# Who copies a chunk's row numbers into the gather ring: GpSimd in place of ScalarE

## The reference, cut to what matters

```python
agg = segment_sum(x[src], edge_type * N_NODES + dst)      # 8 x 3125 rows of 256
h   = act(einsum('rnd,rde->ne', agg.reshape(8, N, D), W) + x @ root + bias)
```

## Time and profile before

| | |
|---|---|
| median of three runs | 4742.41 us (4733.30 to 4748.82) |
| span of the profiled execution | 4717.6 us |
| median less span | 24.8 us |
| GpSimd busy | 2426.4 us, 51% of the span |
| TensorE busy | 2893.6 us, 61% |
| VectorE busy, ScalarE busy | 1194.6 us and 443.2 us |
| mean granted TensorE clock | 0.767 |

### The profile page before, as it was taken

The page is one execution under the profiler, slowest core; times in us unless marked ns, Lnnn a source line. Parts: engine busy times, 40 slices in busy tenths (PEclk is TensorE's granted clock), DMA queues, the critical chain, the costliest instruction groups (busy, mean ns, idle before and its releaser), DMA issues. The chain is left out here.

```text
span 4717.6 us, 51616 instructions
## 1 busy us (share of the span) xinstructions
PE 2893.6 (61%) x16304; PEld 2587.3 (55%) x16304; DVE 1194.6 (25%) x2874; ACT 443.2 (9%) x1230; POOL 2426.4 (51%) x2564
## 2 busy tenths in 40 slices
PE   2556555555556556655656565656767666767786
PEld 2555555545555445545545464555656566666675
DVE  4222222222222122212212122323333233333322
ACT  1000000000000000000000000001111111111132
POOL 5655555555554555555555545665544444444333
PEclk8777777777777776777777777777878778778898
DMA  6333333333333222222222223323443444444576
GB/s 159 108 97 97 99 98 100 100 100 97 101 106 112 84 76 76 84 80 77 81 81 80 81 66 103 87 86 113 134 149 116 132 136 128 142 136 130 169 240 208
DMA packets 276981, 524.37 MB, mean 111 GB/s; under 512 B 60783, under 2 KB 180331, under 8 KB 276716
## 3 DMA queue, kind: packets, MB, share of 16 engines
q0 software_dynamic: 121152, 331.40, 24.3%
q1 hardware_dynamic: 154396, 190.17, 12.7%
q10 hardware_dynamic: 1296, 1.24, 0.1%
HBM read 458.71 MB, written 63.91 MB: 111 GB/s over the span
## 5 line engine op out<-in xcount | busy, mean ns | idle before, releaser
L677 POOL DMA_INDIRECT arena<-rows_dram,arena x2396 | 2273.7, 949 | 1924.7 <-ACT arena L826 1173.3
L1868 PE MATMUL bank<-arena 128*128 128x128 f32 x4836 | 921.4, 320 | 741.3 <-issue 377.2
L1868 PEld LDWEIGHTS bank<-arena 128*128 128x128 f32 x4836 | 821.1, 229 | 833.9 <-issue 509.2
L1463 DVE TENSOR_TENSOR arena<-arena,bank 128x256 f32 x807 | 339.7, 421 | 2690.7 <-remote 1766.8
L1872 PE MATMUL bank<-arena 128*128 128x128 f32 x4836 | 819.5, 309 | 122.9 <-issue 121.8
L1872 PEld LDWEIGHTS bank<-arena 128*128 128x128 f32 x4836 | 733.2, 223 | 134.2 <-issue 133.8
L1723 PE MATMUL bank<-arena 128*128 128x256 f32 x2400 | 632.6, 405 | 171.0 <-DVE zcol L1358 103.3
L1723 PEld LDWEIGHTS bank<-arena 128*128 128x128 f32 x2400 | 463.6, 206 | 236.7 <-issue 182.5
L1385 DVE TENSOR_TENSOR arena<-bank,arena 128x1408 f32<-128x1408 f32 x222 | 355.5, 1604 | 13.1 <-issue 11.6
L1788 PE MATMUL bank<-arena 128*128 128x256 f32 x576 | 203.7, 530 | 151.4 <-ACT arena L904 119.2
L1788 PEld LDWEIGHTS bank<-arena 128*128 128x128 f32 x576 | 157.0, 280 | 191.5 <-issue 157.7
(11 more groups left out here) (230 smaller groups left out, 1529.1 us busy)
## 6 DMA issues: line engine op xcount, KB each, us to landing
arena<-in_L_ffn_W_dram SPq DMA_DIRECT2D x112, 512.0 KB
arena<-in_L_ffn_W_dram SPq DMA_DIRECT2D x44, 1024.0 KB
arena<-rows_dram,arena POOLq DMA_INDIRECT x2418
xs_dram<-zslot SPq DMA_DIRECT2D x25, 1224.0 KB
arena<-xs_dram SPq DMA_DIRECT2D x56, 136.0 KB
rows_dram<-arena SPq DMA_DIRECT2D x50, 128.0 KB
arena<-in_L_gnn_weights_dram SPq DMA_DIRECT2D x6, 1024.0 KB
arena<-ys_dram SPq DMA_DIRECT2D x8, 640.0 KB, 7.8
```

Of the source, the lines that this page charges most:

```text
L677: nc.gpsimd.indirect_dma_start(out=gath[:, slot, :], out_offset=None, in_=rows_dram[l], in_offset=bass.IndirectOffsetOnAxis(ap=idx_ring[:, ...
L1463: nc.vector.tensor_tensor(acc, acc, edge_bank(l, s, q)[:, 0:KD * WC].rearrange("p (k r n) -> p k r n", k=KD, r=REL), ALU.add).then_inc(S[" ...
L1868: nc.tensor.matmul(edge_bank(l, s, q)[:, 0:WC], gath[:, slot, 0:P], onehot[:, slot, :], start=first, stop=last)
```

## The change

GpSimd's stream gets a `ring` of its own: it waits for `group_mm` itself (and in front of chunk C at the start of layers 1 and 2 for `miss_mm`), copies the chunk's row numbers to the ring with `nc.gpsimd.tensor_copy`, raises `ix_ready`, and then waits for `ix_ready` as before, ahead of the gathers. ScalarE's `ring`, its calls, and the copies L997, L1002 and L1006 go. Chunks 0 and 1 of the first layer stay with ScalarE. VectorE's wait for `ix_ready` (L1427) stays.

```diff
@@ gpsimd
                 with pool.If(outside < 1):
                     wait(pool, "rows_st", 16 * (NT - 1) * l)
 
+                    def ring(s, a, n):
+
+                        used = -(-CH * (a + 1) // GT)
+                        if is_first(s):
+                            freed = GROUPS * (l - 1) + (SG * (NSPAN - 1) - (-CH // GT) if a == 0 else GROUPS) if l > 0 else 0
+                        else:
+                            freed = GROUPS * l + SG * (s.m - 1) + used
+                        wait(pool, "group_mm", freed)
+                        if l > 0 and is_first(s) and a == CPS - 1:
+                            wait(pool, "miss_mm", l)
+                        part = idx_part if l > 0 and is_first(s) and a == 0 else idx_i[:, bass.ds(CH * (CPS * s.m + a), n)]
+                        nc.gpsimd.tensor_copy(idx_ring[:, CH * a:CH * a + n], part).then_inc(S["ix_ready"], 1)
+
                     def span(s):
                         for a, n in chunks_of(s):
                             if l == 0 and is_first(s) and a < AHEAD:
                                 continue
+                            ring(s, a, n)
                             if l > 0 and is_first(s) and a == 1:
 
                                 wait(pool, "last_st", 16 * l)
@@ scalar
-            def ring(l, s, a, half, n):
-
-                q = CPS * s.m + a
-                used = -(-CH * (half + 1) // GT)
-                wait(act, "group_mm", GROUPS * l + (SG * (s.m - 1) + used if a < CPS and not is_first(s) else SG * s.m + used if a >= CPS else 0))
-                nc.scalar.copy(idx_ring[:, CH * half:CH * half + n], idx_i[:, bass.ds(CH * q, n)]).then_inc(S["ix_ready"], 1)
-
@@ scalar, span
-                        if is_first(s):
-                            if l == 0:
-                                for a in range(AHEAD, CPS):
-                                    ring(l, s, a, a, CH)
-                            if l == 1:
-                                mix_exp()
+                        if is_first(s) and l == 1:
+                            mix_exp()
...
-                            if u % CH == CH - 1 and not is_last(s):
-                                a = u // CH
-                                if not (is_int(s.m, NSPAN - 2) and a == 2):
-                                    ring(l, s, a + CPS, a, LAST_CHUNK if is_int(s.m, NSPAN - 2) and a == 1 else CH)
-
@@ scalar, end of layers 0 and 1
                         hidden_rows(l, NT - 2)
-                        wait(act, "group_mm", GROUPS * l + SG * (NSPAN - 1) - (-CH // GT))
-                        nc.scalar.copy(idx_ring[:, 0:CH], idx_part).then_inc(S["ix_ready"], 1)
                         turned_back(l, NT - 2)
                         if l == 1:
                             q_stage(NT - 2)
-                        wait(act, "group_mm", GROUPS * (l + 1))
-                        nc.scalar.copy(idx_ring[:, CH:2 * CH], idx_i[:, CH:2 * CH]).then_inc(S["ix_ready"], 1)
                         hidden_rows(l, NT - 1)
                         act.wait_ge(S["miss_mm"], l + 1)
                         nc.scalar.copy(missed[0:LAST, :], bank[NODE_BANK][0:LAST, :]).then_inc(S["miss_out"], 1)
-                        nc.scalar.copy(idx_ring[:, 2 * CH:3 * CH], idx_i[:, 2 * CH:3 * CH]).then_inc(S["ix_ready"], 1)
                         turned_back(l, NT - 1)
```

## The result

The changed kernel took 4622.16 us (median of 4 runs, 4590.40 to 4638.40), the kernel before 4743.06 beside it (4 runs, 4733.30 to 4748.82). The ratio is 0.9719, 95% interval 0.9680 to 0.9758: faster by 2.8%. The prediction said 4781 us and slower. Later runs showed something the prediction had no place for. On two other chips the same kernel before takes 3384 us instead of some 4700, and on one of them the change was measured: it makes the kernel 4.8% slower there. The document first follows the pair of traces that the prediction was about, then the experiments on both sorts of chip.

A forecast was written before the change was run, and what follows sets the result against it. No engine is full; a loop of waits sets the pace, with handovers waiting for TensorE's groups. Waiting chunks +5, ready chunks +39, ScalarE's order -5 made +39 on 4742.4: 4781 us, own range 4757 to 4835, 8-in-10 range 4715 to 4840.

The forecast's parts named there:

- What a waiting chunk pays: GpSimd's handover at 169 chunks that wait for TensorE's group: 1.13 us before, 1.13 to 1.18 after; +5 us in all.
- What a ready chunk pays: 51 chunks with row numbers already copied, nearly all a span's third: 1.06 us for 0.30 ahead of the gather; +39 us.
- Does each delay reach the end?: A span's three chunks stand in one chain, so a microsecond lost ahead of the third lengthens the span by one.
- held add: VectorE's add of a group computed long before; it was seen 3.30 us behind the third chunk's last gather.
- first rival: Pause ahead of a span's third chunk pays for itself: -83 us, 4659; 14 in 100 clear gain, 20 no change.
- ScalarE's order: Copies held up behind gelus in layer 2 and a copy of `missed` at layer starts are freed: together -5 us.

The follow-up runs named there:

- e10: The changed kernel, unaltered, run again on a late chip beside the kernel before: 4435.94 us, ratio 0.966.
- e12: Changed kernel with the third chunk's row numbers copied during the second, so no pause ahead of a ready third chunk; late chip: 4582.12 us, 0.998.
- e18: Changed kernel with the third chunk's row numbers copied and waited for after the second chunk's sixth gather; late chip: 4549.74 us, 0.966.
- e16: The changed kernel, unaltered, run on a prompt chip beside the kernel before: 3547.95 us, ratio 1.048.
- e2: Changed kernel with ScalarE still waiting for the groups at its old places, without copying: 4649.15 us, 0.979.
- e1: Kernel before plus one GpSimd copy into unused columns and a wait for it ahead of each span's third chunk: 4717.14 us, 0.991.
- e3: Changed kernel with GpSimd copying each chunk's row numbers during the chunk before, into two rings, without pauses: 4682.23 us, 0.986.
- e11: Kernel of e3 plus a GpSimd copy and wait ahead of each span's third chunk, on a late chip: 4492.56 us, 0.977.
- e13: Changed kernel plus a GpSimd copy and wait after the fifth gather of every chunk, on a prompt chip: 3701.45 us, 1.094.
- e7: Changed kernel with the third chunk's row numbers copied during the second, so no pause ahead of it; prompt chip: 3502.76 us, 1.035.
- e4: Changed kernel plus a second GpSimd copy and wait ahead of each span's third chunk: 4616.71 us, 0.970.

## Why the prediction was wrong

**The prices were right.** "What a waiting chunk pays": 1.13 us, forecast 1.13 to 1.18 after, and the group that ends at 1900.69 is followed by the gather at 1901.88, 1.19 behind. "What a ready chunk pays": forecast 1.06 us in front of C, measured 0.96 in layer 0 and 1.04 in layer 1, so +0.66 to +0.74 instead of +0.76. The 0.09 us that I had put ahead of the copy is not there: the copy starts where the gather ends.

**The step that failed is "Does each delay reach the end?"**, in its last sentence but one: "a microsecond lost ahead of C is a microsecond on the span". It took the distance from C's last gather to the held add as fixed. On late chips that distance is what the pause shortens (e10 against e12), and in the first pair, while 46 pauses cost 32 us, the handovers behind them gave back 110. The first rival had this mechanism, with 14 in 100 for a clear gain and 4659 us as its end; the measured 4622 lies beyond even that. Against it I had held that the pause was seen once, and that 1.06 us is shorter than the 2.3 us after which held groups were seen. The second argument was wrong: the pause need not be long enough for the signal to come inside it. In e18 it ends 16 us ahead of the add that it advances. And the effect had been measured too small: the earlier trace rows is the third group's add, 2.30 us behind C's last gather, but the earlier trace rows is the second group's, 3.30 behind; the third group's stood 4.12 behind.

**The same step is right on a prompt chip.** There VectorE's adds follow their groups, all three chunks are ready, and the forecast price of 0.76 us on 220 chunks would be +167 us. Measured: +163 (3384.65 to 3547.95). That they meet so closely is partly luck: the traces show some 0.70 us a chunk, 154 us, and the kernel before has no trace on such a chip to show where the rest is. The trace that I read had the sign of the chip in it: VectorE waiting for something that the profile could not name. That row of the kernel before, of the changed kernel, and of e16 on a prompt chip:

```profile
DVE arena L1463 <- remote: 1766.8, 218, 19.3
```

```profile
DVE arena L1456 <- remote: 1710.9, 243, 15.2
```

```profile
DVE arena L1456 <- PE bank L1865: 1771.6, 637, 11.6
```

I wrote that I did not know why the groups' semaphores are seen so late, and went on to price the change as if the lateness were a constant. A wait whose cause is unknown should have had both bounds in the sum: held fast, +39; moved by the change, -83 or more. The range (4715 to 4840) reached only part of the way to the second.

**ScalarE's order** was forecast at -5 us. By e2 it may be as much as 30 on a late chip, a quarter of the gain; the intervals do not tell the two apart, and the two ratios are from two chips.

**What stays open.** Why a pause ahead of C is worth 3.2% between e12 and e10, but only 0.9% on the kernel before (e1) and 0.8% between e3 and e11 (two chips). These differ in who copies at A's and B's handover, and no run changed that alone. Breaks in every chunk (e13) were not measured on a late chip. The changed kernel ran on two late chips and on one prompt chip, and the prompt one has no trace of the kernel before. And why late chips are late is not shown.

## What to carry to other kernels

Where an engine stands idle although its producer's work is recorded as long done, find out what the wait follows before pricing a change by it. Here it followed the bursts of gathers, and for pauses of 0.7 us in bursts of 22 three times their length came back. Time such a change on more than one chip: this one is worth -2.8 and -3.4% on two late chips and +4.8% on a prompt one, and a tuning that fits one sort undoes the other. Where nothing is held, a copy and an own wait in GpSimd's stream cost 0.7 us for each chunk, and the relay over an idle ScalarE costs nothing.

## What the runs showed of the hardware that I had not expected

Two sorts of chips, or of states of them. On chips 2 and 4 the kernel before took 3381 to 3386 us, elsewhere 4567 to 4778. Instructions last the same on both: a gather on GpSimd 0.952 us in the changed kernel's first trace and 0.950 in e7's, an add 0.421 in both. TensorE is busy 2900.6 us in the changed kernel's first trace and 2892.8 in e16's, so its granted clock (0.766 and 0.844 in the mean) is not the difference. The difference is in the signals. On a late chip the mean lag from group to add is 4.8 to 6.8 us in layers 0 and 1, up to 25; on a prompt one 0.3, at most 1.7 (in layer 2 4 to 5 on the one and 1.0 on the other). The late traces also hold fewer records of signals: 16,756 semaphore updates in the kernel before and 17,151 in the changed one, 52,634 in e16. The row of the gathers in the list of DMA issues (count, then the median time to landing where there is one), of the changed kernel on a late and then on a prompt chip:

```profile
arena<-rows_dram,arena POOLq DMA_INDIRECT x2418
```

```profile
arena<-rows_dram,arena POOLq DMA_INDIRECT x2418, 2.8
```

The records that are there say more (my counts; the numbers are of the changed kernel, late and then prompt, in e16). What is missing is above all landings of gathers: 8,324 of 38,688 are there against 38,640. The rows themselves come as fast on both: from a gather's start to the end of its last DMA packet it takes 2.42 us at the median of layers 0 and 1, and to the recorded rises of its landing 2.49 and 2.62. Of the groups' semaphore, which is what comes late, 742 of 807 rises are there. Over all semaphores that TensorE alone raises, 561 of 1,313 recorded rises follow the recorded end of an instruction within 0.1 us, against 1,392 of 1,412. VectorE's are never late: 1,849 of 1,885 against 2,387 of 2,423, and the 36 left over are about one for each semaphore on both. So neither the data nor VectorE is late on a late chip. TensorE's rises are (or TensorE itself, as its ends are modelled), and they are not the ones whose records are missing.

The Trainium skill has a rule that bears on this: NOTIFIC — the notification-queue block, section 7.1 "Overflow: three behaviours, one of which stalls the engine", says that a full queue of records drops new ones, overwrites old ones or stalls their producer, and that the block's inner stages hold their producers back rather than lose a record. By that rule the lateness could come from the recording itself, which bursts of landings would fill and pauses would drain. The missing records agree with it as far as they go; that VectorE's rises are on time, though a fifth of their records is missing, is not explained by it. No run here shows it, since every timed run carries a record of its span, and the page also says that its authors never saw either overflow mark set.

A GpSimd copy of 128x11 int32 lasts 0.19 to 0.21 us and starts within 0.01 us of the end of the gather before it. The gather behind it starts 0.77 to 0.86 us after the copy's end where it waits for the copy's semaphore; where it does not, as in e12, 0.16 us (L726 there). A second copy that waits for the first starts 0.14 us behind its end (e4). That answers what the prediction left open beside the Trainium skill's GPSIMD Engine Reference, section 2.1 "Instruction dispatch": the semaphore that the rule asks for between a Pool write and a Pool reader costs 0.6 us in front of a gather, where the earlier trace rows had 0.09 between plain operations.
